# Reciprocal roots of the q and k norms all on VectorE, with new batch openings and last attention steps

## The reference

```python
def reference(x, Wq, Wk, Wv, Wo, q_norm_w, k_norm_w, w_gate, w_up, w_down):
    # x (2, 1024, 512); 32 query heads, 8 kv heads of 128; inner size 1376
    xn = layernorm(x)
    q, k, v = xn @ Wq.T, xn @ Wk.T, xn @ Wv.T
    q = q * rsqrt(mean(q * q) + 1e-6) * q_norm_w      # per head
    k = k * rsqrt(mean(k * k) + 1e-6) * k_norm_w
    scores = q @ k.T / sqrt(128) + slope[head] * (j - i)   # j <= i, else -1e30
    s = (softmax(scores) @ v) @ Wo.T
    g = silu((silu(xn @ w_gate.T) * (xn @ w_up.T)) @ w_down.T)
    return x + s * g
```

## Time and profile before

| | |
|---|---|
| median of 3 runs | 2481.81 us (2481.43 to 2482.60) |
| the profiled execution | 2481.58 us, of which 2479.7 us are the span from first to last instruction |
| TensorE matmuls busy | 2432.2 us, 98% of the span |
| VectorE busy | 1680.3 us, 68% |
| ScalarE busy | 1234.7 us, 50% |
| GpSimd busy | 778.2 us, 31% |
| mean granted TensorE clock | 0.996 of full speed |
| DMA | 92.19 MB, mean 37 GB/s |

### The profile page before, as it was taken

How to read it: one execution, slowest core, us unless ns; L and a number is a source line. 1 busy time by engine, 2 the same in 40 slices (tenths; PEclk the granted TensorE clock), 3 DMA queues, 4 the chain that set the end, 5 groups by cost and what they waited for, 6 DMA issues and landing times.

```text
span 2479.7 us, 37446 instructions
## 1 busy us (share of the span) xinstructions
PE 2432.2 (98%) x13232; PEld 2063.4 (83%) x13232; DVE 1680.3 (68%) x3709; ACT 1234.7 (50%) x2548; POOL 778.2 (31%) x2154
## 2 busy tenths in 40 slices
PE   6999999999999999999989999999999999999998
PEld 5888888888888888788878888888888888887887
DVE  5777777777868687723267777777777777777132
ACT  3555554555545555533345555555554555545333
POOL 4323241413233223144533232323231414231443
PEclk9999999999999999999999999999999999999999
DMA  3000000000000000023320101010000000010223
GB/s 125 5 27 18 26 18 26 18 26 18 26 18 26 18 27 18 26 78 135 110 77 1 43 1 43 1 36 8 26 18 26 18 26 18 1 43 14 90 96 108
DMA packets 22841, 92.19 MB, mean 37 GB/s; under 512 B 6528, under 2 KB 6656, under 8 KB 18560
## 3 DMA queue, kind: packets, MB, share of 16 engines
q1 hardware_dynamic: 22656, 89.80, 10.5%
HBM read 85.60 MB, written 4.19 MB: 36 GB/s over the span
## 4 chain that ended last, share of the span: by engine, by line
PE 95%; DVE 2%; ACT 1%; issue 1%; DMA 0%; POOL 0%; SPq 0%; DVEq 0%; POOLq 0%; ACTq 0%
PE score_ps L325 16%; PE out_ps L349 16%; PE out_ps L362 14%; PE qkv_ps L299 14%; PE ring_ps L336 10%; PE qkv_ps L300 7%; PE score_ps L432 5%; PE qkv_ps L432 5%; PE ring_ps L447 3%; PE ring_ps L307 2%; PE out_ps L447 1%; PE ring_ps L312 1%; PE score_ps L299 0%; DMA qkv_raw<-w_qkv_dram 0%; DVE y L838 0%
## 5 line engine op out<-in xcount | busy, mean ns | idle before, releaser
L518 ACT ACTIVATE pT_hi<-ring_ps 128x512 fp32r<-128x512 f32 x576 | 343.8, 599 | 524.1 <-PE ring_ps L336 512.9
L694 DVE TENSOR_TENSOR pT_lo<-ring_ps,pT_hi 128x512 fp32r<-128x512 f32 x576 | 395.9, 689 | 91.8 <-ACT pT_hi L518 88.1
L510 ACT ACTIVATE probs<-probs,low_min 128x896 f32<-128x896 f32 (+7 forms) x512 | 394.7, 772 | 44.8 <-DVE low_min L686 44.5
L857 POOL TENSOR_SCALAR rs_x<-sq_sum 128x5 f32<-128x5 f32 x128 | 25.3, 198 | 1134.5 <-DVE sq_sum L654 1134.5
L336 PE MATMUL ring_ps<-ident,probs 128*128 128x128 f32 x2304 | 347.2, 274 | 1.0 <-DVE probs L704 1.0
L686 DVE CUSTOM_DVE_ANT_0 probs<-score_ps,rel_sb,slope 128x512 f32<-128x512 f32 (+3 forms) x512 | 329.7, 645 | 8.9 <-PE score_ps L325 5.6
L336 PEld LDWEIGHTS ring_ps<-ident,probs 128*128 128x128 f32 x2304 | 278.6, 141 | 51.2 <-issue 1.6
L325 PE MATMUL score_ps<-kv_hi,qT_hi 128*128 128x512 f32 (+3 forms) x768 | 278.5, 363 | 12.0 <-DVE kv_lo L672 6.4
L349 PE MATMUL out_ps<-pT_hi,kv_hi 128*128 128x512 f32 x576 | 266.1, 462 | 2.4 <-DVE pT_lo L694 2.0
L325 PE MATMUL score_ps<-kv_hi,qT_lo 128*128 128x512 f32 (+3 forms) x768 | 266.7, 347 | 0.0
L325 PE MATMUL score_ps<-kv_lo,qT_hi 128*128 128x512 f32 (+3 forms) x768 | 265.1, 345 | 0.0
(11 more groups left out here) (136 smaller groups left out, 5411.5 us busy)
## 6 DMA issues: line engine op xcount, KB each, us to landing
qkv_raw<-w_ffn_dram SPq DMA_DIRECT2D x44, 768.0 KB, 4.2
qkv_raw<-w_qkv_dram SPq DMA_DIRECT2D x16, 1536.0 KB, 6.7
o_raw<-w_o_dram SPq DMA_DIRECT2D x16, 1024.0 KB, 4.8
probs<-x_dram SPq DMA_DIRECT2D x4, 1024.0 KB, 7.2
o_raw<-x_dram SPq DMA_DIRECT2D x4, 1024.0 KB, 6.5
out_dram<-y SPq DMA_DIRECT2D x16, 256.0 KB, 3.8
rel_sb<-rel_dram SPq DMA_DIRECT2D x1, 512.0 KB, 11.3
inv_slope<-inv_slopes_dram SPq DMA_DIRECT2D x16, 2.5 KB, 1.7
```

The costliest lines, as they stand in the source:

```text
L510: act.activation(row, row, ACT.Exp, scale=-1.0, bias=low_min[:, i % 2, h, HEAD_CHUNKS[i] - 1:HEAD_CHUNKS[i]], accum_out=row_sum[:, i % 2, ...
L518: act.activation(pT_hi[:, n % SLOTS, :], ring_ps[:, ring_bank(r), :], ACT.Copy).then_inc(ring_high, 1)
L694: dve.tensor_tensor(out=pT_lo[:, n % SLOTS, :], in0=ring_ps[:, ring_bank(r), :], in1=pT_hi[:, n % SLOTS, :].bitcast(F32), op=ALU.subtract) ...
```

## The change

- For tile numbers with `early(t)` true, `sum_squares` on VectorE is followed at once by the reciprocal root there: nine instructions that each wait for the one before (EARLY_CHAIN = 9), and a tenth that writes rq. EARLY is UNITS * TILES = 64. GpSimd calls `norms` only where `early` is false.
- Start of the kernel: x comes in three pieces (tiles 0 and 1, 2 and 3, 4 to 7), the weights of unit 0 in four; the norms of x of the first batch are made on VectorE; only tiles 0 and 1 are transposed before the first projection, the others behind the second.
- Openings of both batches: the third projection goes ahead of the first scores, which use out_ps and a ring bank instead of score_ps.
- Second batch: x's norms and both halves' normalising go into the last chunks of the FFN before it.
- Last unit of a batch: the last `exp` of steps 5, 6 and 7 goes behind the copy of the attention output; q and k of the next tile are transposed two slots earlier in steps 5 and 6; the gate half of chunk 0 goes ahead of step 7, its up half ahead of step 8, the gate half of chunk 1 ahead of step 9. For this there is a third slot for gate/up weights, and gate and up swap PSUM banks.

```diff
-CHAINS = UNITS * TILES + HALVES
+EARLY = UNITS * TILES
+CHAINS = UNITS * TILES - EARLY + HALVES
...
+EARLY_CHAIN = 9
+FIRST_X = (0, 2, HT, TILES)
...
+def turn_qk_at(i, turns, last):
+
+    return turns - 1 if last and i >= TILES - 3 else turns + 1
...
+        gu_hi, gu_lo = [[own[:, :]] + [w[:, k * NGU:(k + 1) * NGU] for k in range(2)]
...
-        gate_ps = [score_ps[:, k, :] for k in range(2)]
-        up_ps = [qkv_ps[:, k * BANK:(k + 1) * BANK] for k in range(2)]
...
+        gate_ps, up_ps = [[banks[part] for banks in (qkv_banks, score_banks)] for part in range(2)]
...
+        first_xT_ps = down_ps + down_ps
+        xT_ps = score_banks + qkv_banks + down_ps
...
+        def score_of(n, width, first):
+
+            if first and n < G:
+                return out_ps[:, 0:width] if n % 2 == 0 else ring_ps[:, ring_bank(1), 0:width]
+            return score_ps[:, n % 2, 0:width]
+
+        def early(t):
+
+            return (t - 1) % (UNITS * TILES) < EARLY
...
+            load_first_x(0)
+            for c in range(DC):
+                sp.dma_start(qkv_raw[:, c, :], w_qkv[0:1, :, c * NW:(c + 1) * NW].rearrange("a p n -> p (a n)")
+                             ).then_inc(first_w_in[c], 16)
+                if c == 0:
+                    sp.dma_start(ident[:, :], ident_in).then_inc(ident_loaded, 16)
+                if c == 1:
+                    load_first_x(1)
+            load_first_x(2)
...
+                    pe.wait_ge(v_staged, tile(U, 0))
+                    project(U, 2, first_ps, True)
                     for k in range(G):
                         scores(U, 0, k, True)
-                    pe.wait_ge(biased, U * SCORES + G)
-                    project(U, 2, first_ps, True)
                     turn_q(U, 1, RING_AT[0] + BEFORE[0], True, tile(U, 1))
...
-                    if ahead and turns and k == turns + 1:
+                    if ahead and turns and k == turn_qk_at(i, turns, last):
...
+                if t >= HT and row == 0:
+                    pe.wait_ge(xT_low, t - HT + 1)
+                elif t >= HT:
+                    pe.wait_ge(gate_done, (row - 1) * TILES + t + 1)
...
-                        for i in range(HT, TILES):
-                            turn_x(b, i)
-                        pe.wait_ge(xT_low, b * TILES + HT)
+                        if b:
+                            for i in range(HT, TILES):
+                                turn_x(b, i)
+                            pe.wait_ge(xT_low, b * TILES + HT)
                         project(U, 1, qkv_ps, True)
+                        if b == 0:
+                            for i in range(FIRST_X[1], TILES):
+                                turn_x(b, i)
...
-                        if i == TILES + 1:
-                            gate_up(0, 0, 0)
+                        if last and i >= TILES - 1:
+                            c, part = divmod(i - TILES + 1, 2)
+                            gate_up(c, c, 0, range(part, part + 1))
...
+                        square(first_ps, tile(U, 2), False)
+                        stage_v(first_ps, 2, tile(U, 2), True)
+                        high_q(U, 1, RING_AT[0] + BEFORE[0])
+                        high_k(U, 1, RING_AT[0] + BEFORE[0] + 1)
                         for h in range(G):
                             exp(U, 0, h)
-                        high_q(U, 1, RING_AT[0] + BEFORE[0])
-                        high_k(U, 1, RING_AT[0] + BEFORE[0] + 1)
-                        square(first_ps, tile(U, 2), False)
-                        stage_v(first_ps, 2, tile(U, 2), True)
                         high_o(U, 0, False)
                         high_o(U, 1, False)
...
+                    if last and i >= TILES - 2 and i <= TILES:
+                        exp(U, i - 1, G - 1)
                     if i > TILES:
-                        high_gate_up(1, 1)
...
-                        if 1 <= k <= chunks and k % HEAD_CHUNKS[i] == 0:
+                        if 1 <= k <= chunks and k % HEAD_CHUNKS[i] == 0 and not (last and i >= TILES - 3 and k == chunks):
...
+                        if last and i == TILES - 2 and k == turns:
+                            high_gate_up(0, 0)
                         if i == TILES and k == LAG + 1:
-                            high_gate_up(0, 0)
+                            high_gate_up(1, 1)
...
+                if early(t):
+                    dve.wait_ge(summed, t)
+                    b, nth = divmod(t - 1, UNITS * TILES)
+                    if nth % TILES == 0:
+                        dve.wait_ge(inv_in, (b * UNITS + nth // TILES + 1) * 16)
+                    early_rsqrt(sq_sum[:, :], slice(0, G + 1), 1.0 / P, RMS_EPS, 2 + b * EARLY + nth)
+                    dve.scalar_tensor_tensor(out=rq[:, :], in0=early_y[:, 0:G + 1], scalar=0.375, in1=inv_slope[:, :],
+                                             op0=ALU.mult, op1=ALU.mult).then_inc(rq_done, 1)
+
+            def early_rsqrt(src, at, mul, add, nth):
+
+                xx, aa, yy = early_x[:, at], early_a[:, at], early_y[:, at]
+                done = nth * EARLY_CHAIN
+
+                def chained(ins, count):
+                    ins.then_inc(early_chain, 1)
+                    dve.wait_ge(early_chain, done + count)
+
+                chained(dve.tensor_scalar(xx, src, mul, add, ALU.mult, ALU.add), 1)
+                chained(dve.tensor_scalar(yy.bitcast(I32), xx.bitcast(I32), -0.5, RSQRT_SEED, ALU.mult, ALU.add), 2)
+
+                chained(dve.tensor_tensor(out=aa, in0=yy, in1=yy, op=ALU.mult), 3)
+                chained(dve.scalar_tensor_tensor(out=aa, in0=aa, scalar=-RSQRT_C1, in1=xx, op0=ALU.mult, op1=ALU.mult), 4)
+                chained(dve.scalar_tensor_tensor(out=yy, in0=aa, scalar=RSQRT_C0, in1=yy, op0=ALU.add, op1=ALU.mult), 5)
+
+                chained(dve.tensor_tensor(out=aa, in0=yy, in1=yy, op=ALU.mult), 6)
+                chained(dve.tensor_tensor(out=aa, in0=aa, in1=xx, op=ALU.mult), 7)
+                chained(dve.scalar_tensor_tensor(out=aa, in0=aa, scalar=-1.25 / 0.375, in1=aa, op0=ALU.add, op1=ALU.mult), 8)
+                chained(dve.scalar_tensor_tensor(out=yy, in0=aa, scalar=1.875 / 0.375, in1=yy, op0=ALU.add, op1=ALU.mult), 9)
 
...
+            def early_x_norms(nth, lo, hi):
+                dve.wait_ge(mv_done, hi)
+                early_rsqrt(mv[:, lo:hi, 1], slice(lo, hi), 1.0, LN_EPS, nth)
+                dve.tensor_scalar(rs_y[:, lo:hi], early_y[:, lo:hi], 0.375, None, ALU.mult).then_inc(x_rs_done, 1)
+                dve.wait_ge(x_rs_done, nth + 1)
+
+            dve.wait_ge(first_x_in[0], 16)
+            tile_stats(0, 0, FIRST_X[1])
+            early_x_norms(0, 0, FIRST_X[1])
+            normalise_x(0, 0, FIRST_X[1])
+            dve.wait_ge(first_x_in[1], 16)
...
+                        scale_qk(qkv_ps, 1, tile(U, 1))
                         for k in range(G):
-                            bias(U, 0, k)
-                        scale_qk(qkv_ps, 1, tile(U, 1))
+                            bias(U, 0, k, True)
+                        sum_squares(tile(U, 2), False)
                         low_q(U, 1, RING_AT[0] + BEFORE[0])
                         low_k(U, 1, RING_AT[0] + BEFORE[0] + 1)
-                        sum_squares(tile(U, 2), False)
                         scale_qk(first_ps, 0, tile(U, 2))
...
-                        normalise_x(b, 1)
                         sum_squares(tile(U, 0), True)
-                        for t in range(HT, TILES):
+                        if b == 0:
+                            normalise_x(b, FIRST_X[2], FIRST_X[3])
+                        for t in range(HT if b else FIRST_X[1], TILES):
...
-                    if not (last and i >= TILES - 2):
+                    if not (last and i >= TILES - 2) and not early(tile(U, i + 2)):
...
+                    if last and i == TILES - 2:
+                        low_gate_up(0, 0)
 
                 def unit(U, first, last):
-                    if first:
-                        norms(U, 0)
-                        norms(U, 1)
                     for i in range(TILES + 2 if last else TILES):
                         step(U, i, first, last)
```

More of the change, by code:

```diff
@@ L181, in build, with xT_bank @@
         o_parts = [slice(k * 2 * D, (k + 1) * 2 * D) for k in range(2)]
+        def xT_bank(row, t):
+            return (xT_ps if row else first_xT_ps)[t]
+        def score_of(n, width, first):
[4 more added lines that the diff above has]
+            return (t - 1) % (UNITS * TILES) < EARLY
         def tile(U, i):
@@ L454, in chunk @@
                         return
-                    gate_up(c, k, half)
+                    gate_up(c, k, half, range(1, 2) if c == 1 else range(2))
                     down(c - 1, 1 - k)
@@ L673, in low_k, with bias @@
                                   in1=kT_hi[:, i * P:(i + 1) * P].bitcast(F32), op=ALU.subtract).then_inc(ring_lowd, 1)
-            def bias(U, i, k):
+            def bias(U, i, k, first=False):
                 n = SCORE_AT[i] + k
```

(9 more changed lines are left out.)

130 lines of the change are left out of this document (76 added, 54 removed).

## The result

| | before | after |
|---|---|---|
| median of the timed runs, us | 2481.62 (2481.25 to 2482.6, 4 runs) | 2546.41 (2545.14 to 2547.5, 4 runs) |
| ratio | | 1.0262, 95% interval 1.0249 to 1.0274 |
| profiled execution / its span, us | 2481.58 / 2479.7 | 2546.05 / 2544.2 |

The forecast was 2505, with a range of 2474 to 2540. The sign was right and the time lies outside the range, 41 us above the forecast.

The account below looks back on a forecast made before the run. TensorE was taken to set the time, busy 127.98 of 128.00 us per mid-batch unit. Chain 42, clearing of y 3, openings -6 and -5, last steps -10.5 sum to +23.5 on 2481.58: 2505 us, range 2474 to 2540.

Parts of the forecast that it names:

- The chain: Root on VectorE after each tile's reduction: delays biases and scale_qk that TensorE waits for; 42 us plus 3 for clearing y.
- the link: One dependent small VectorE instruction of the root's nine; taken as 0.18 us, between 0.16 and 0.20.
- the halving: Steps 0 and 2 of a unit: only half the computed delay counted, 0.5 us together, ends 0 and 0.98.
- The clearing of y: First unit's step 2: it stands behind the chain too, leaving no slack; 1.4 us more per batch, 3 in all.
- The openings: Start of each batch: the new order gains 6 us (0 to 12) in the first, 5 (0 to 8) in the second.
- the costs in DMA are none that I see: Openings: six more issues on SP in the first microseconds, no queue that compute waits on later; no cost.
- the line that ends an opening: Tile 3's reduction, chain and division on VectorE before step 1's first turned probabilities; put at 44 and 1273.7 us.
- The last steps: End of a batch's attention: gate/up matmuls moved ahead of steps 7, 8 and 9 cover waits; gain 10.5 us, 4 to 13.
- the 70: The 70 us window ending a batch's attention: TensorE idle 6.0 us before, under 2 expected after.
- (a): Faster rival: VectorE's free time absorbs the chain unfelt by TensorE, only parts 2 and 3 count; 2460 us, chance 0.15.
- (b): Same-time rival: a link costs 0.14 to 0.15 us, stalls of some 20 us equal the gains; chance 0.07.
- (c): Much slower rival: links of 0.21 us or more, or GpSimd's long splits hold up one chain per unit; 2539 us, chance 0.1.

Follow-up runs that it names:

- wcol_late: The changed kernel with wcol and its wait for the norm weights' transfer moved behind the first two tiles' splits of x; 2546.0 us, ratio 1.0252.
- early2: The changed kernel with EARLY = 2: only a batch's first two tiles keep the chain on VectorE, all others use GpSimd; 2476.4 us, ratio 0.9978.
- gate_high_early: The changed kernel with ScalarE rounding the first gate weights in slot 1 of step 6 of a batch's last unit, not its last slot but one; 2542.5 us.
- links7: The changed kernel with two of the nine links left out, so its output differs; 2510.2 us, ratio 1.0113.
- links11: The changed kernel with two further links whose result nobody reads; 2595.7 us, ratio 1.0454.
- chain_slot0: The changed kernel with the ten links moved behind the first slot's bias and split of the turned probabilities, the reduction staying at the step's head; 2808.0 us.

## Why the prediction was right in sign and wrong in size

**The chain (predicted 45, measured 61).** The mechanism was right, a chain that delays the first bias for which the third scores wait. The term that was off is the link: 0.18 was taken as the middle of 0.16 to 0.20, and it is 0.20 in the trace, the upper end. The row nearest to a link was the reciprocal, with its successor 0.20 behind it; that row should have been taken, not a mean with a one-element instruction that nothing waits for. For 0.20 the prediction's own sum gives 59 + 4 = 63. By steps, the lengths between projections in a unit before and after:

| step | 0 | 1 | 2 | 3 | 4 | 5 | 6 | 7 | unit |
|---|---|---|---|---|---|---|---|---|---|
| before | 17.96 | 10.44 | 12.36 | 13.60 | 16.07 | 17.39 | 19.22 | 21.04 | 128.08 |
| after | 18.54 | 11.23 | 12.58 | 13.83 | 16.53 | 18.09 | 20.06 | 21.23 | 132.09 |
| lost | 0.58 | 0.79 | 0.22 | 0.23 | 0.46 | 0.70 | 0.84 | 0.19 | 4.01 |
| predicted | 0.3 | 0.8 | 0.2 | 0 | 0.35 | 0.53 | 0.65 | 0 | 2.8 |

Each of steps 3 to 7 lost 0.11 to 0.23 more than predicted, about the 0.19 by which the chain is longer. In step 0 the halving was wrong too: the whole 0.58 arrives. In step 1 the size was right but not the place. The forecast had TensorE idle before the next projection, released by `scale_qk`. In the trace it is idle before the third scores and before the first weighing, and the next projection follows at 588.56 without idle time:

```profile
586.65 0.69 DVE L810 TENSOR_TENSOR y<-out_ps,y 128x512 f32<-128x512 f32 x1
...
587.43 0.47 PE L389 MATMUL out_ps<-pT_hi,kv_hi 128*128 128x512 f32 x1 [0.48 <-issue]
```

That weighing waits in the program for `add_y` and starts 0.09 behind its end. That 0.8 came out there owes something to luck. The clearing of y came as predicted: over step 2 of the first unit the lag grows by 1.6, of which 0.2 are the step's own loss and 1.4 the clearing.

**The openings (predicted -6 and -5, measured +4.6 and +0.4).** Two steps failed. First, "the costs in DMA are none that I see". The wait for the norm weights stood ahead of the splits on VectorE, and their transfers are now issued behind eight others (three of x, four of the weights, the identity) where it was two:

```profile
14.51 0.16 DVE L842 SCALAR_TENSOR_TENSOR wcol<-norm_w 128x1 f32<-128x1 f32 x1 [3.74 <-DMA norm_w<-k_norm_dram]
```

The first projection came at 17.78, not at 13. With that wait moved back it came at 13.96 in wcol_late's trace. The forecast saw the six further issues and did not ask who waits for the transfers behind them. Second, the line that ends an opening, the chain of tile 3 and the divisions. It was seen, and priced at an undisturbed 44 and 1273.7. It came at 53.92 in the first batch, 9.9 late. Of these 4.8 are the first projection's, 2.0 the first link's behind GpSimd's split, 0.5 other links', and 2.6 stay open. In the second batch the first turned probabilities stood, with the lag of 32.8 that it had at the batch's first projection taken off, at 1278.6 (1311.34 - 32.75), 4.9 late: 2.09 for the reduction's wait on ScalarE, 2.16 for the first link behind GpSimd's split, and some 0.5 for links of up to 0.31 beside GpSimd's smaller instructions (2.20 from the second link's start to the instruction behind the chain, where step 0 above has 1.68). early2, with that chain on GpSimd again, has the 5 us. So the new order can give what was forecast for the second batch, but not with the chain on VectorE, where the forecast had counted it.

**The last steps (predicted -10.5, measured -1.5).** The forecast's sign was under 2 us idle in the 70, and it was over 3. The sentence that failed is "the cover needs ScalarE's and GpSimd's split of that chunk in time, and both have gaps there". ScalarE has gaps, but its order puts the rounding into step 6's last slots, and 1.0 of ScalarE plus 2.4 of GpSimd end 1.99 us after TensorE is there, in both batches. gate_high_early shows it: with the rounding earlier the two stretches are together 7.6 shorter than before (254.9 to 250.4, 258.7 to 255.6). The same cover, given its input in time, is worth 7.6 of the 10.5; the other 2.9 were not looked for.

**The sum.** 16 for the chain, 16 for the openings (5.0 instead of -11) and 9 for the last steps are the 41 us of the miss.

**The rivals.** (a), no loss from the chain, fell with links7 and links11: nearly every further link arrives at the end. (b) fell with the link of 0.20. (c), at 2539, came nearer to the time than the forecast, but for the most part not for its reasons. The links were 0.20, not 0.21. GpSimd's long splits did hold up a chain, but once a batch and not once a unit: the first links of the 128 chains (L738) took 28.3 us together, 6.3 more than at 0.172 each, and 4.2 of that are the two openings. "Mostly past the chain" held in mid-unit; chain_slot0 shows what it costs where it does not hold.

## What to carry to other kernels

A chain of dependent small instructions is priced by its start-to-start time from the nearest row that has a dependent successor, and by what stands behind it on its engine. Such a chain belongs where the engine that sets the time has the longest stretch of work that needs nothing of this one, and where this one would itself have to wait; a share of idle time says nothing of that place. Work put in as cover is only cover if each of its inputs, on every engine and queue, is there when it starts: read the last-arriving input of each filler before counting its gain.

## What the runs showed of the hardware

- **VectorE waits for GpSimd as GpSimd does for VectorE.** The trace of before showed one direction. Here some of VectorE's instructions lasted about until GpSimd's running one ended: 2.33 and 2.17 instead of 0.17 for a link (TENSOR_SCALAR), 2.27 for one with two inputs in SBUF, 5.11 instead of 0.88 for four divisions. Not all are held up. In the changed kernel's first opening GpSimd's two splits run from 46.35 to 51.0; beside them L753 (an input in PSUM) took its 0.81 and the reduction its 0.82, and the link behind it 2.17:

```profile
46.37 0.81 DVE L753 TENSOR_TENSOR natural<-score_ps,rq 128x640 f32<-128x640 f32 x1
48.03 0.82 DVE L718 TENSOR_REDUCE sq_sum<-natural 128x5 f32<-128x640 f32 x1 [0.85 <-ACT natural L545]
48.89 2.17 DVE L738 TENSOR_SCALAR early_x<-sq_sum 128x5 f32<-128x5 f32 x1
```

  The Trainium skill, SBUF — State Buffer, section Who interferes with whom, sorts them so: a reduction never contends, an instruction with one input in SBUF doesn't unless it is of a kind that can enter a two-port mode (tensor_scalar is one), two inputs in SBUF do. The three rows agree.
- **A short wait went with a slow clock behind it, but not always.** Behind 1.99 us of idle time the 12 matmuls of a gate half took 3.07 us in one batch, 0.39 for most of them, at a granted clock of 1.00. In the other they took 4.42, from the seventh on 0.63 each, and the clock from 2323 to 2326 us was 0.52, close to the lower of its two levels. Nine profiles have this wait (1.99 to 2.02 us) in both batches: the 12 matmuls took 3.06 or 3.07 in seven of these 18 places and 4.33 to 4.62 in eleven. In the three kernels with the rounding in slot 1 there is no wait, and they took 2.96 in all six, again from the start of the first to the end of the last (2.79 without the overlap with the matmul before). So removing 1.99 us of waiting took 2.3 us off one stretch and 3.9 off the other.
- **The first opening is not the same in every execution.** With the same code ahead of it, the first projection started between 17.8 and 20.1 us in the profiles. VectorE's wait for the norm weights' transfer was 3.74 us in the earliest and 5.65 in the latest. A gain of 2 us there needs many timed runs.
